# Three equal blocks in every slot, a lag of three, and weights laid out beforehand, in a three-stage decoder layer

## The chip, the cores and the metric

One core of a Trainium2 chip runs the whole program. Its engines are TensorE (PE; its weight loads are shown apart as PEld), VectorE (DVE), ScalarE (ACT), GpSimd (POOL) and SyncE (SP), which only issues transfers here. The metric is the device time of one execution in microseconds (us), as the median over runs; lower is better.

## What is computed

The input x has 16 batches of 128 rows of 256 numbers. Three blocks follow one another, each on the layer-normed x and added to x:

```python
x = x + attn(layernorm(x))          # 16 heads of 64; q, k, v, dots, weights, out are cut to 1/4096 and clipped at 8
x = x + xattn(layernorm(x), ctx)    # 16 heads; keys and values from a context of 128 rows of 128
x = x + ffn(layernorm(x))           # two experts share wi (1024) and wo; each adds a rank-16 product inside the relu
```

The first attention cuts every intermediate to fixed point (`trunc(clip(t) * 4096) / 4096`): q, k, v, the scores, the softmax weights, the attended values and the projection.

## The kernel before, in words

**Numbers.** Matrix products need more precision than one pass of rounded operands gives, so each operand is split in a rounded high part (`_hi`) and a low part (`_lo`, raw minus high), and a product is three matmuls (`split3`, lines 402 to 407: weights low by moving high and so on). A weight matrix must thus be transposed where its layout asks for it, rounded, and subtracted.

**Tiling.** Four groups of four batches (512 tokens). Stage A is the first attention, stage B the attention to the context, stage C the feed-forward part. In A and B a group is eight slots, a slot is two heads; in C a slot is 128 of the 1024 hidden columns. Each engine has its own program, and all walk through the same slots (`a_slot`, `b_slot`, `c_slot` in each engine's block); the first group is written out, the other three are a loop. The order inside a slot is written by hand for each engine, and counting semaphores tie the engines together. Each engine takes its instructions in strict order.

**Stage A, PE (lines 505 to 531).** A slot n makes the q block and the k block (128 weight columns by 512 tokens, six matmuls of 512 columns each, into PSUM banks `proj_ps[m % 2]`); transposes the weights of slot n-2 (`a_transpose`, L464); adds slot n-3's part to the output projection (`project_out`, 12 matmuls of 256 columns); attends for slot n-2 (`a_attend`, L475); in slots 0 to 3 only, makes two value blocks (`a_block`, one batch by 512 value columns each); and makes the scores (`a_scores`, L498). In slot 7 the next group's normalised rows are transposed (`normed_T`, L438) between projection and attend. So a slot has four blocks in 0 to 3 and two in 4 to 7 (`block_index`, lines 69 to 74).

**Stage A, the others.** Each block's result goes to ACT for its sign (`sign_of`, L804) and to DVE, which subtracts half the sign and writes int16 (`fix_blocks`, L1021), then clips (L1025). The bank is free when the integers are written (`a_ri`). Scores: sign (L851), integers (L1116), clip (L1120), exponential with sums (ACT, L819), reciprocal (DVE, L1047), then GpSimd makes the integer weights p_int (L311, L316), PE transposes them, ACT makes `aT_sb` of them (L809), and only behind that, on ACT, come the next slot's exponentials. `e_sb`, `p_int`, `rsum` and `rsc` are single. After the attend: sign (L826), integers (L1037), high part (L1040), low part (L1042). DVE also does the layer norm of the next group (L966, L978, L985, L1013) and the last rounding of the projection (`y_out` L1056, `fix_y` L1065 to L1071), GpSimd the root of the variance (L304, L306) and the sum into x (L325).

**Stage B** (PE lines 614 to 683, DVE 1147 to 1227) works alike without fixed point: maxima (L1164), negated (L1168), exponentials (ACT, L889), reciprocal (L1199), GpSimd's p_f (L363), transposes (L583), DVE's copies (L1175), attend (L595), high part on ACT (L900), low part on DVE (L1206). All blocks (q, value, k, value) go through one PSUM bank, `one_ps`: q is copied out by ACT (L875), k and values by DVE (L1145, L1137), each before the next block. A slot's order on PE is q, transposes, value, projection, k, attend, value, scores; slots 4 to 7 have no value blocks. Each group starts with four transposes of the context (L621).

**Weights.** Stage A's (`w_qkv`, `w_proj`) come in rows; PE transposes them (`a_weights_T`, L426) in 16 pieces, ACT rounds each to the high part (L791), DVE makes the low part (L1005); eight pieces stand before the first rows. The first DMA on SP's queue is 512 KB of these weights, the second the first group's rows. Stage B's high parts are converted by GpSimd's own DMAs (L343), the raw ones come through `raw_b`, and GpSimd subtracts (L351), in groups 0 and 1. Stage C's are transposed between B and C in 13 pieces (`c_weights`, lines 691 to 716, 910 to 929, 1237 to 1260), with the drain slots of stage B among them.

## Time and profile before

| | |
|---|---|
| runs | 730.95 us median of 3 (729.81 to 731.84) |
| profiled execution, span | 730.2 us; its own time is not given apart from the three runs, the median is 0.75 us above the span |
| busy share of the span | PE 92%, PEld 76%, DVE 75%, ACT 57%, POOL 37% |
| data moved in the first 1/40 of the span | 312 GB/s |
| DMA | 18.75 MB in all |

PE's busy time is from the start of a matmul to a modelled end, so that matmuls overlap in it; the distance between the starts of two matmuls tells what one costs. An idle time stands in brackets behind an instruction, with the engine and the instruction that ended it.

### The profile page before, as it was taken

Reading aid. Unit: us, or ns where it says so; the run is one execution under the profiler, and the core shown is the slowest. Engines: PE = TensorE matmul, PEld = TensorE weight load, DVE = VectorE, ACT = ScalarE, POOL = GpSimd, SP = SyncE. Lnnn points to the kernel's source line nnn. Section 1 sums busy time; section 2 is a strip of 40 time slices with the busy share of each in tenths; the row PEclk is TensorE's granted clock in tenths of the full one; section 3 lists DMA queues with packets and bytes.
Section 4 is the critical chain, followed back from the end, with each engine's and each line's share of the span. In section 5 each row is a group of like instructions: output and inputs, shape, how many; then the busy total and the mean of one; then the engine's idle time right before and its main releaser. Section 6 shows DMA issues by size and latency. Waiting matters only on the chain.

```text
span 730.2 us, 15676 instructions
## 1 busy us (share of the span) xinstructions
PE 672.8 (92%) x5186; PEld 551.7 (76%) x5186; DVE 550.0 (75%) x1142; ACT 413.7 (57%) x1443; POOL 272.6 (37%) x610
## 2 busy tenths in 40 slices
PE   5998879989998899878989999999999889999997
PEld 4777768777886788766777877787788777888986
DVE  5879887887888789757767776677667668787775
ACT  4677756767776777764455455445544563433432
POOL 1166754454445534535354344234333532010110
PEclk9999999999999999999999999999999999999999
DMA  9135100000000000050000000000000000000000
GB/s 312 49 111 150 60 30 1 1 1 1 0 0 0 0 0 0 0 153 1 1 2 16 1 1 1 14 0 0 0 0 0 0 1 1 2 30 0 29 29 29
DMA packets 17002, 18.75 MB, mean 26 GB/s; under 512 B 2851, under 2 KB 15427, under 8 KB 16963
## 3 DMA queue, kind: packets, MB, share of 16 engines
q1 hardware_dynamic: 15330, 15.11, 6.4%
q0 software_dynamic: 1632, 3.15, 1.5%
q8 instruction: 21, 0.34, 0.2%
q14 instruction: 19, 0.15, 0.1%
HBM read 16.16 MB, written 2.10 MB: 25 GB/s over the span
## 4 chain that ended last, share of the span: by engine, by line
PE 35%; POOL 7%; DVE 6%; ACT 3%; issue 3%; DVEq 0%; POOLq 0%; ACTq 0%
PE bank L405 9%; PE bank L407 8%; PE bank L406 8%; POOL p_f L363 6%; PE bank L583 3%; ACT e_sb L889 2%; PE bank L595 2%; PE bank L607 1%; DVE mx L1164 1%; PE bank L729 1%; PE bank L741 1%; DVE bn_st L966 1%; DVE oT_lo L1206 1%; POOL p_int L316 0%; DVE v_sb L1137 0%
## 5 line engine op out<-in xcount | busy, mean ns | idle before, releaser
L363 POOL TENSOR_SCALAR p_f<-e_sb,rsum 128x128 f32<-128x128 f32 x256 | 95.6, 398 | 156.7 <-DVE rsum L1199 156.7
L316 POOL TENSOR_SCALAR p_int<-e_sb,rsc 128x128 int16<-128x128 f32 x256 | 116.2, 475 | 6.3 <-issue 5.7
L889 ACT ACTIVATE e_sb<-bank,neg_max 128x128 f32<-128x128 f32 x256 | 90.1, 380 | 12.1 <-DVE neg_max L1168 11.9
L804 ACT ACTIVATE sgn<-bank 128x512 bf16<-128x512 f32 x96 | 57.2, 598 | 57.6 <-PE bank L407 57.6
L819 ACT ACTIVATE e_sb<-si 128x128 f32<-128x128 int16 x256 | 75.1, 303 | 0.0
L1021 DVE SCALAR_TENSOR_TENSOR ri<-sgn,bank 128x512 int16<-128x512 bf16 x96 | 62.5, 677 | 7.3 <-ACT sgn L804 6.5
L875 ACT COPY q_sb<-bank 128x512 f32<-128x512 f32 x32 | 18.8, 587 | 84.5 <-PE bank L407 84.5
L311 POOL TENSOR_TENSOR rsc<-rsum,growth 128x8 f32<-128x8 f32 x32 | 6.7, 209 | 156.0 <-DVE rsum L1047 156.0
L889 ACT ACTIVATION_READ_ACCUMULATOR e_sb<-bank,neg_max 128x1 f32 x256 | 55.9, 218 | 0.0
L405 PE MATMUL bank<-xnT_hi,wqkvT_lo 128*128 128x512 f32 x128 | 53.6, 419 | 2.2 <-DVE ri L1021 1.3
L1175 DVE COPY aT_sb<-bank 128x512 f32<-128x512 f32 x64 | 41.2, 685 | 12.7 <-PE bank L583 12.5
L407 PE MATMUL bank<-xnT_hi,wqkvT_hi 128*128 128x512 f32 x128 | 50.2, 392 | 0.0
L406 PE MATMUL bank<-xnT_lo,wqkvT_hi 128*128 128x512 f32 x128 | 49.9, 390 | 0.0
L819 ACT ACTIVATION_READ_ACCUMULATOR e_sb<-si 128x1 f32 x256 | 49.9, 195 | 0.0
L809 ACT ACTIVATE aT_sb<-bank 128x1024 f32<-128x1024 int16 x32 | 32.8, 1026 | 25.6 <-PE bank L464 25.6
L1145 DVE COPY k_sb<-bank 128x512 f32<-128x512 f32 x32 | 22.1, 691 | 30.0 <-PE bank L407 30.0
L583 PE MATMUL bank<-ident,p_f 128*128 128x128 f32 x256 | 34.1, 276 | 11.3 <-POOL p_f L363 10.5
L583 PEld LDWEIGHTS bank<-ident,p_f 128*128 128x128 f32 x256 | 28.5, 140 | 20.1 <-POOL p_f L363 15.4
L950 ACT CAST oT_hi<-hid 128x512 fp32r<-128x512 f32 x32 | 19.9, 622 | 41.0 <-DVE hid L1282 41.0
L1164 DVE TENSOR_REDUCE mx<-bank 128x4 f32<-128x512 f32 x64 | 40.8, 677 | 0.4
L464 PE MATMUL bank<-ident_b,p_int 128*128 128x128 bf16 x256 | 19.8, 220 | 22.7 <-POOL p_int L316 22.7
L405 PE MATMUL bank<-wpT_hi,oT_lo 128*128 128x256 f32 x128 | 39.1, 305 | 1.8 <-DVE oT_lo L1042 1.8
(162 smaller groups left out, 2039.5 us busy)
## 6 DMA issues: line engine op xcount, KB each, us to landing
x_sb<-in_x SPq DMA_DIRECT2D x4, 512.0 KB, 10.3
wqkv_raw<-in_L_attn_w_qkv SPq DMA_DIRECT2D x2, 1024.0 KB, 10.2
out<-x_sb SPq DMA_DIRECT2D x8, 256.0 KB, 2.2
wqkv_raw<-in_L_attn_w_qkv SPq DMA_DIRECT2D x2, 512.0 KB, 5.1
wp_raw<-in_L_attn_w_proj SPq DMA_DIRECT2D x1, 1024.0 KB, 12.3
raw_b<-in_L_xattn_Wq SPq DMA_DIRECT2D x2, 512.0 KB, 3.3
wq_hi<-in_L_xattn_Wq POOLq DMA_DIRECT2D x2, 512.0 KB, 4.1
wo_hi<-in_L_xattn_Wo POOLq DMA_DIRECT2D x2, 512.0 KB, 8.4
```

Source lines behind the costliest of these rows:

```text
L316: i = nc.gpsimd.tensor_scalar(p_int[:, t, :], e_sb[:, t, :], rsc[:, t:t + 1], -0.5, ALU.mult, ALU.add)
L363: i = nc.gpsimd.tensor_scalar(p_f[:, t, :], e_sb[:, t, :], rsum[:, t:t + 1], 0.0, ALU.mult, ALU.add)
L405: pe.matmul(out_, wl, mh, start=first, stop=False, **kw)
L406: pe.matmul(out_, wh, ml, start=False, stop=False, **kw)
L407: return pe.matmul(out_, wh, mh, start=False, stop=last, **kw)
L583: last = pe.transpose(pT_ps[hh][:, b * P:(b + 1) * P], p_f[:, GB * hh + b, :], ident[:, :])
L804: nc.scalar.activation(sgn[:, m % 2, :], proj_ps[m % 2][:, :], ACT.Sign).then_inc(a_sgn, 1)
L819: last = nc.scalar.activation(e_sb[:, t, :], si[:, i, j * P:(j + 1) * P], ACT.Exp, scale=1.0 / FIX, accum_out=sums[:, t:t + 1])
L889: last = nc.scalar.activation(e_sb[:, t, :], s_ps[hh][:, (t % 4) * P:(t % 4 + 1) * P], ACT.Exp, bias=neg_max[:, t:t + 1], scale=DH ** -0.5 ...
L1021: V.scalar_tensor_tensor(ri[:, i, :], sgn[:, i, :], -0.5, proj_ps[i][:, :], ALU.mult, ALU.add).then_inc(a_ri, 1)
L1164: V.reduce_max(mx[:, half], s_ps[hh][:, :].rearrange("p (a t) -> p a t", a=GB), AX).then_inc(b_mx, 1)
L1175: i = V.tensor_copy(aT_sb[:, GB * hh:GB * hh + GB, :].rearrange("p a t -> p (a t)"), pT_ps[hh][:, :])
```

## The change

In stages A and B every slot now makes three blocks: q, k and one value block, which is a quarter of the value columns (256) for two batches, side by side in one bank. Transposes and attend are for the slot three back (`LAG`), the projection for the slot four back, and `e_sb`, `p_int`, `p_f`, `rsum` and `rsc` are double. The host lays out the weights and the context transposed, so that no weight or context is transposed on PE; high parts come by GpSimd's DMAs (the first q, k and value pieces are rounded on ACT), low parts are made by GpSimd in halves of 512 (A) or pieces of 1024 (B and C, and the low rank factors). The scale of 4096 goes from the weights to the norm factor of the rows (one more small GpSimd product). The first group's rows are the first DMAs, on two queues, and PE runs 14 matmuls on zeros before anything has landed.

PE, stage A and B:

```diff
-    return 4 * s if s < 4 else 16 + 2 * (s - 4)
-BLOCKS = block_index(8)
+BLOCKS = 3 * NP
+LAG = 3
...
+            for _ in range(14):
+                pe.matmul(t_ps[:, :], warm[:, 0:P], warm[:, :], start=True, stop=True)
...
+            def a_rows(g, s):
+                m = 3 * s + 2
+                a_block_free(g, m)
+                for i in range(2):
+                    b = 2 * (s % 2) + i
+                    for kt in range(KD):
+                        last = split3(proj_ps[m % 2][:, i * QW:(i + 1) * QW],
+                                      [t[:, kt, b * P:(b + 1) * P] for t in (xnT_hi, xnT_lo)],
+                                      [w[:, s // 2, kt, :] for w in (wv_hi, wv_lo)], i == 0 and kt == 0, kt == KD - 1,
+                                      skip_group_check=True)
+                last.then_inc(a_blk, 1)
...
-                a_block(g, base, s * P, True)
-                a_block(g, base + 1, E + s * P, True)
...
-                    a_transpose(n - 2)
-                if not (first and s < 3):
-                    project_out(n - 3, (s - 3) % NP, a_olo, a_pj, (wpT_hi, wpT_lo), (a_z, 2 * g))
+                for i in range(2):
+                    a_block(g, 3 * s + i, [w[:, s, :, i, :] for w in (wqk_hi, wqk_lo)])
+                lagged = not (first and s < LAG)
+                if lagged:
+                    a_transpose(n - LAG, (s - LAG) % 2)
...
+                a_rows(g, s)
+                if lagged:
...
+                    a_attend(n - LAG, p, BLOCKS * gg + 6 * (p // 2) + 6)
                 if s == NP - 1:
-
                     normed_T(g + 1, lambda: wait(pe, a_ri, BLOCKS * (g + 1)))
...
+                    project_out(n - LAG - 1, p, a_olo, a_pj, (wp_hi, wp_lo), (a_z, 2 * g))
+                a_scores(n, s, BLOCKS * g + 3 * s + 2)
...
+                    b_block(g, s, "q")
+                    transposes()
+                    b_block(g, s, "v")
+                    project((0, 1))
+                    b_block(g, s, "k")
+                    project((2, 3))
+                if s == NP - 1:
...
+                    normed_T(G + g + 1, free)
+                attend()
+                b_scores(g, n, s)
...
-            for s in range(2):
+            for s in range(LAG):
                 b_slot(G, s, drain=True)
```

GpSimd, and the queues:

```diff
+            for b in range(2):
+                sp.dma_start(x_sb[:, b, :], x[b]).then_inc(ld_x0[b], 16)
+            sp.dma_start(wqk_raw[:, 0, :, :, :], wqk[:, 0, :, :, :]).then_inc(ld_qk[0], 16)
...
+            for b in range(2, GB):
+                nc.scalar.dma_start(x_sb[:, b, :], x[b]).then_inc(ld_x0[b], 16)
...
+                nc.gpsimd.tensor_tensor(lo, raw, hi.bitcast(F32), ALU.subtract).then_inc(w_lo, 1)
...
+            for part in LOW_ORDER[1:6]:
+                load_high(*part)
...
+            inv_std(0, scaled=True)
+            pool.wait_ge(ln_xn, 1)
+            for part in LOW_ORDER[0:3]:
+                make_low(*part)
...
+                if not first and s in (3, 6):
+                    chunk = 2 * (g - 1) + (s - 3) // 3
...
+                    nc.gpsimd.tensor_tensor(lo, raw, hi.bitcast(F32), ALU.subtract).then_inc(wB_done, 1)
...
+                    nc.gpsimd.tensor_tensor(wi_lo[:, s - 1, :], wi_raw[:, s - 1, :], wi_hi[:, s - 1, :].bitcast(F32),
+                                            ALU.subtract).then_inc(cw_lo, 1)
...
+                    nc.gpsimd.tensor_tensor(wd_lo[:, half, :], wd_raw[:, half, :], wd_hi[:, half, :].bitcast(F32),
+                                            ALU.subtract).then_inc(cw_lo, 1)
```

ACT and DVE, stage A (the high part of the attended values goes from DVE, L1040, to ACT):

```diff
+                    a_exp(n - 1, (s - 1) % 2, 0)
+                sign_of(g, 3 * s + 2)
+                if lagged:
+                    a_out_sign(n - LAG)
+                if s == NP - 1:
+                    xnT_high(g + 1)
+                if not (first and s == 0):
+                    a_exp(n - 1, (s - 1) % 2, 1)
+                if lagged:
+                    a_out_high(n - LAG)
...
                 between_groups(g, s, first)
+                to_int(g, 3 * s + 2)
...
+                    a_out(n - LAG)
+                clipped(g, 3 * s + 2, v_rows(s), ri[:, s % 2, :].rearrange("p (a c) -> p a c", a=2), 1.0)
                 if s == NP - 1:
                     xnT_low(g + 1)
                 if not (first and s == 0):
-                    a_recip(n - 1)
...
+                    a_recip(n - 1, (s - 1) % 2)
+                if lagged:
+                    a_out_low(n - LAG)
+                if s == LAG and not first:
                     y_out(g)
```

## Rows read from the trace of the kernel before

**Rows 1.** The page, busy time and instructions of each engine.
```profile
PE 672.8 (92%) x5186; PEld 551.7 (76%) x5186; DVE 550.0 (75%) x1142; ACT 413.7 (57%) x1443; POOL 272.6 (37%) x610
```

**Rows 2.** Timeline of PE: start us, us, instruction; row transposes, then stage C's first matmul.
```profile
14.78 1.52 PE L438 MATMUL bank<-ident,xn 128*128 128x128 f32 x8
...
86.32 0.93 PE L438 MATMUL bank<-ident,xn 128*128 128x128 f32 x7
...
165.23 1.04 PE L438 MATMUL bank<-ident,xn 128*128 128x128 f32 x8
...
314.59 1.04 PE L438 MATMUL bank<-ident,xn 128*128 128x128 f32 x8
...
388.63 1.09 PE L438 MATMUL bank<-ident,xn 128*128 128x128 f32 x8
...
586.77 1.09 PE L438 MATMUL bank<-ident,xn 128*128 128x128 f32 x8
...
609.13 0.47 PE L405 MATMUL bank<-xnT_hi,wiT_lo 128*128 128x512 f32 x1
```

**Rows 3.** Timeline of PE, one slot with values and one without, stage A.
```profile
202.88 0.62 PE L464 MATMUL bank<-ident_b,p_int 128*128 128x128 bf16 x8
203.31 0.36 PE L405 MATMUL bank<-wpT_hi,oT_lo 128*128 128x256 f32 x1
...
204.91 1.09 PE L475 MATMUL bank<-aT_sb,v_sb 128*64 128x128 f32 x16
205.93 0.50 PE L405 MATMUL bank<-wqkvT_hi,xnT_lo 128*128 128x512 f32 x1
...
208.92 1.16 PE L498 MATMUL bank<-k_sb,q_sb 64*128 64x128 f32 x16
...
212.91 0.62 PE L464 MATMUL bank<-ident_b,p_int 128*128 128x128 bf16 x8
...
221.29 0.62 PE L464 MATMUL bank<-ident_b,p_int 128*128 128x128 bf16 x8 [1.20 <-POOL p_int L316]
```

**Rows 4.** Timeline of POOL and DVE near 85; then line 1282: min/median/max ns, first and last start.
```profile
84.30 2.39 POOL L351 TENSOR_TENSOR wv_lo<-raw_b,wv_hi 128x1024 fp32r<-128x1024 f32 x1
...
85.29 1.68 DVE L1025 TENSOR_SCALAR q_sb<-ri 128x512 f32<-128x512 int16 x1
86.89 0.41 DVE L1025 TENSOR_SCALAR k_sb<-ri 128x512 f32<-128x512 int16 x1
...
L1282 DVE SCALAR_TENSOR_TENSOR hid<-relu,top_sb,hid x32: 741/750/822, 614.2 to 722.2; 128x512 f32<-128x512 f32 x32
```

**Rows 5.** Timeline of PE, the stall in group 1 of stage A.
```profile
106.70 0.62 PE L464 MATMUL bank<-ident_b,p_int 128*128 128x128 bf16 x8 [2.69 <-POOL p_int L316]
```

**Rows 6.** Timeline of PE, from transposes to transposes, a slot without values, stage B.
```profile
427.94 1.03 PE L583 MATMUL bank<-ident,p_f 128*128 128x128 f32 x8
...
435.63 1.10 PE L583 MATMUL bank<-ident,p_f 128*128 128x128 f32 x8 [0.81 <-POOL p_f L363]
```

**Rows 7.** Timeline of PE and DVE, the loop of a slot with values, stage B.
```profile
405.49 0.44 PE L405 MATMUL bank<-cT_hi,wk_lo 128*128 128x512 f32 x1
...
406.32 1.10 PE L595 MATMUL bank<-aT_sb,v_sb 128*64 128x128 f32 x16
...
408.96 0.68 DVE L1206 TENSOR_TENSOR oT_lo<-bank,oT_hi 128x512 fp32r<-128x512 f32 x1
...
410.21 1.27 DVE L1164 TENSOR_REDUCE mx<-bank 128x4 f32<-128x512 f32 x2
...
413.13 0.68 DVE L1137 COPY v_sb<-bank 128x512 f32<-128x512 f32 x1
...
413.93 0.44 PE L405 MATMUL bank<-cT_hi,wk_lo 128*128 128x512 f32 x1
```

**Rows 8.** Timeline of DVE, the first rows' statistics and their normalisation.
```profile
5.84 1.40 DVE L966 BATCH_NORM_STATS2 bn_st<-x_sb 128x6 f32<-128x256 f32 x4 [5.84 <-DMA x_sb<-in_x]
...
9.26 1.38 DVE L985 TENSOR_SCALAR xn<-x_sb,mv,rstd 128x256 f32<-128x256 f32 x4 [1.59 <-POOL rstd L306]
```

862 lines of the change are left out of this document (401 added, 461 removed).

## The prediction, made before the changed kernel was run

> **What bounds the kernel now.** I read the page first: TensorE (PE) is busy for 672.8 us, 92% of the span [rows 1]. That only says that PE is close everywhere, so I next cut the span into stages by one landmark, the transposes of the next group's normalised rows, which stand once in each group's pass [rows 2]. The first pass of stage A takes 86.32 - 14.78 = 71.5 us, the second 78.9, the next two together 149.4 (74.7 each); the first pass of stage B 74.0, the next three 198.1 (66.05 each); from the last landmark of stage B to the first matmul of stage C are 22.4 us. Stage C is not changed and its PE is never free, so it counts nothing.
>
> In a stage A group the first four slots take 10.03 us and have no gap; the last four wait for GpSimd's weights, 1.20 us in the slot shown (8.38 us long) [rows 3]. Three of these and one like it at the next group's first slot are all that lags can win: about 4.9 us a group. In stage B the gap before the transposes of an attend-only slot is 0.81 us [rows 6], while the slots with values run at the pace of a loop through VectorE (DVE): value copy, k block, attend, rounding, maxima, copies, next value copy; k to k is 8.44 us [rows 7].
>
> **Stage A, a slot of the new kernel.** The slot keeps everything of a 10.03 us slot but the two value blocks (12 matmuls of 512 columns, 2.99 us); it gets 12 of 256 columns. The projection is 12 matmuls of 256 columns and takes 1.60 us with its changeover [rows 3], and I take that. New slot: 10.03 - 2.99 + 1.60 = 8.64 us of pure PE. Eight of them and the landmark's 1.0: 70.1, where the old group has 74.7 - 4.9 = 69.8. So quarters cost PE 0.3 a group, and the gain is the gap alone. The Trainium skill, TensorE: Matmul & The Clock Gate, section Back-to-back issue gap, gives N/2.4 + 2.5 ns per matmul, 109 ns at 256 columns; by it twelve take 1.31 us, the slot 8.35, and four groups of stage A 9 us less. The row has 1.60, and the sum goes by the row.
>
> Where do new waits come from? A bank is free again after DVE has made integers of it, and with three blocks in two banks the value block of a slot waits for that slot's own q. By passes of 0.6 us, scores, sign, integers, clip and then q's integers end some 4.3 us after the scores' start, which is q's start + 3.2; PE comes there at +3.3. It holds with nothing to spare. Four things eat into it. The rows' transposes now stand behind the attend and need the last value block's integers: 1.05 us a group. The two output passes after the fourth slot's rounding: 0.75. The longer norm work of the second and fifth slot: 0.1. And GpSimd's own weight subtractions, next.
>
> **GpSimd holds DVE.** While GpSimd ran a subtraction of 2.39 us from 84.30, a DVE clip of an SBUF tile that started at 85.29 took 1.68 us where the next one took 0.41, that is, until GpSimd's was over; a DVE operation with two SBUF inputs took at most 0.82 against a median of 0.75 [rows 4]. In the old kernel six such subtractions stand in the first two groups. In the new one there are 14 half-wide ones in group 0, six full ones in groups 1 to 3 (two each, in slots 3 and 6), and some seven in the first pass of stage B. A held clip costs between 0 and 2.4 us; I charge 1.0 each, a little under the 1.27 that the row shows, because some will fall in a gap. Groups 1 to 3 get 2.0 each. The Trainium skill, GPSIMD Engine Reference, section 8. Key points, says that the two engines contend over DVE's two-port mode and over two SBUF inputs; by it roundings and sums would be held too, and the sum would be some 12 us more. By that rule, the trace agrees on the clip, and hardly on the two inputs (0.82 against 0.75).
>
> Sum for a group of A: 70.1 + 1.05 + 0.75 + 0.1 + 2.0 = 74.0. Against 78.9 in group 1, which also has a stall of 2.69 us behind GpSimd's subtractions [rows 5], -4.9. Groups 2 and 3: 148.0 against 149.4, **-1.4**. The cast that goes from DVE to ScalarE (ACT), some 0.5 us, I cost at nothing: ACT has over a microsecond free in such a slot. If that cover went, it would be 0.5 a slot.
>
> **Start and group 0.** Now the rows land at 5.84, behind 512 KB of weights, and DVE's normalised rows are ready at 10.64, but PE is still transposing weights and turns to them only at 14.78 [rows 8, 2]. The weight transposes, the 32 passes of ACT and DVE over their results, and PE's wait go. Rows asked for first should land about 1.6 us earlier (an estimate: 512 KB stand ahead of them, and the page's first slice moved 312 GB/s); one small GpSimd product costs 0.3. The landmark comes at 10.7 - 1.6 + 0.3 = 9.4: **-5.4**. Six DMA issues on GpSimd stand ahead of the root of the variance and should be over before it; if not, this term loses 1 to 3 us. The 14 warming matmuls lie in PE's idle time and cost nothing.
> Group 0: 2.7 to the first q; three slots with no attend, where the scores wait for k's passes, 6.7 each; 7.0 for the fourth (no projection); three of 8.64; 6.95 up to the landmark: 62.6. GpSimd's 14 subtractions of some 1.2 us hold clips while nothing else is slack: +4, bounds 0 to 12. So 67.0 against 71.5, **-4.5**.
>
> **Stage B.** A group has 7.69 - 0.81 = 6.88 us of PE in an attend-only slot [rows 6]; a value block of quarters is six matmuls of 256 columns, 0.80, and the split projection has one more changeover: 7.7. But now every slot has a value copy, and half a projection (0.80) stands between k and attend, inside DVE's loop. The old loop, 8.44, has 0.65 of statistics and a wait of 0.24 in it [rows 7]; without them 7.55. The second value block's copy leaves it: from attend to rounding it took 2.64, where attend, ACT's cast and their latencies need 1.8. New loop: 7.55 + 0.80 - 0.84 = 7.5, and every other DVE pass between rounding and maxima comes on top. By passes of 0.6 (512 wide) and 0.33 (256 wide) these are 0.6, 0.65, 1.85, 0.95, 1.25 and 0.65 in six of the slots. Over 7.7 that is 0.4 + 0.45 + 1.65 + 0.75 + 1.05 + 0.45 = 4.75. A group: 8 x 7.7 + 1.05 + 4.75 = 67.4 against 66.05: three groups **+4.1**. Stage B gets slower: its PE gap goes and a DVE wait takes its place.
> The first pass of B loses its context transposes and their stall, but takes over stage A's last three attends, and gets GpSimd's weight work. Without holds 67 to 68, with seven holds of about 1: 74 to 75 against 74.0: **0**, bounds -7 and +8.
>
> **From B to C.** Now 609.13 - 586.77 = 22.4 us [rows 2], full of the last stage's weight preparation on PE, ACT and DVE. New: 2.05 to the last scores, then maxima, exponentials, reciprocal, GpSimd's weights (8.9 us, in which two drain slots run on PE), transposes, projection, attend, low rank product and last projection, 6.5: 17.5. **-4.9**. Should GpSimd's preparation be late, this term is lost first; it has a whole stage of slack.
>
> **Sum.** -5.4 - 4.5 - 4.9 - 1.4 + 0 + 4.1 - 4.9 = -17.0. The profiled span is 730.2, 0.1% under the runs' median of 730.95; the profiled execution's own time is not given apart, so I put what lies around the span at the difference, 0.75: 730.95 - 17.0 = **714.0 us**. This case's own range is 703 to 725, chance 0.58.
>
> **Rivals.**
> (a) PE stays filled. Holds fall in gaps and DVE's passes fit. Then A groups are 70.1, B groups 62.7, the first passes lose 4 and 5 more: -11.7 - 4 - 14.1 - 5 = -34.8, 679 us. For it: DVE is idle a quarter of the span. Against it: strict order on each engine, and the loops above. Chance 0.13, most of it short of the full gain.
> (b) Slower. The place is the value block's wait for its slot's q. All of DVE's extra passes of a group (some 8.4 us) then lie on the loop, not the 0.85 charged, and a hold costs its whole length: +9 us a group, four times, 750 us. It decides from 0.53 us a slot more than forecast (17.0 over 32 slots). For it: the loop has 0.1 us to spare. Against: most extra passes stand where DVE waits for ACT's value sign. Chance 0.12.
> (c) The start doesn't deliver. Raw and rounded copies of 7 MB are asked for at once on three queues; rows or first weights land late. The 5.4 go and group 0 loses 4: 723. Chance 0.10.
> (d) GpSimd's subtractions hold DVE's two-input passes too: each of some 27 then also stops a rounding or sum, for about 0.45 more on average: 726. The row with 0.82 against 0.75 speaks against it [rows 4]. Chance 0.07. It is what the page of the Trainium skill on GPSIMD, named above, would have.
>
> **How the numbers follow.** A difference of 0.3% (2.2 us) is about what can be told from no change. 690 to 733 leaves out most of (b) and the far end of (a). Faster: 0.56 of the forecast's 0.58, all of (a), about 0.13 of (c) and (d) together: 0.82. Within 0.3%: 0.04. Slower: 0.14.
>
> **What the profile after would show.** Right: the first landmark near 9.4; landmarks in stage A 74 apart with slots of 8.6 to 8.7, no wait of transposes for GpSimd, PE's waits being on DVE's integers; clips lengthened to 1 to 2.4 us beside GpSimd's subtractions; stage B's landmarks 67 apart with k waiting for the value copy; 17.5 us from the last to stage C. Wrong: slots of A over 9.2 all along (b), B at 63 (a), a first landmark after 13 (c), long roundings (d).

## The result and the profile after

The changed kernel takes **741.6 us** (median of 4 runs, 739.9 to 742.7) where the kernel before takes 730.8 beside it: ratio 1.0148, 95% interval 1.0133 to 1.0164. I forecast 714.0 with a range of 690 to 733 and gave "slower" 0.14. It is slower, and outside the range.

The page of the profile, busy time by engine, against [rows 1]:

```profile
PE 671.4 (91%) x5358; PEld 569.2 (77%) x5358; DVE 533.4 (72%) x1080; ACT 413.8 (56%) x1445; POOL 307.8 (42%) x656
```

PE is busy 1.4 us less and the span is 9.3 us longer (739.5 against 730.2). The 1.4 hides two things. The mean granted clock fell from 0.995 to 0.979: ahead of the end seven stretches, 30.7 us in all, ran at half clock (1.2 GHz), where a matmul counts for longer; before there were two of 3.4 us. And work did leave PE: kernel 11 below, with the same matmuls and eight more, is busy for 658.1 us at a mean clock of 0.995 again, 14.7 less than before (its order differs too). So what was won on PE went into waits and half clock. Where, the windows between landmarks tell. The columns are: stretch, its length, PE busy (instructions), weight loads, DVE, ACT, POOL, granted clock as a share of the full one, DMA share, GB/s. The rows are the start, stage A's four groups, stage B's four, the passage to C, and C to the end.

```profile
0.00:12.11 12.11, 4.87 (x14) 1.74 (x15) 4.01 (x15) 2.42 (x3) 6.44 (x21) 0.98 0.84 251
12.11:83.47 71.36, 62.65 (x468) 51.66 (x469) 50.81 (x106) 46.62 (x158) 44.47 (x77) 0.91 0.51 190
83.47:160.22 76.75, 71.50 (x617) 61.27 (x617) 62.06 (x127) 57.28 (x194) 36.50 (x78) 0.98 0.01 2
160.22:237.48 77.26, 71.89 (x617) 61.33 (x617) 62.60 (x127) 57.52 (x194) 37.86 (x79) 0.98 0.00 0
237.48:313.20 75.72, 70.39 (x616) 60.06 (x617) 62.49 (x127) 57.43 (x194) 37.86 (x79) 1.00 0.02 4
313.20:392.17 78.97, 66.20 (x540) 55.47 (x541) 52.94 (x103) 40.57 (x163) 48.11 (x96) 0.96 0.18 62
392.17:462.43 70.26, 64.76 (x544) 55.08 (x545) 45.85 (x100) 33.77 (x147) 30.39 (x70) 0.98 0.02 5
462.43:531.15 68.72, 63.21 (x545) 53.82 (x545) 45.73 (x100) 33.88 (x147) 24.72 (x66) 1.00 0.02 4
531.15:599.87 68.72, 63.19 (x544) 53.78 (x545) 45.72 (x100) 33.86 (x147) 24.71 (x66) 1.00 0.00 0
599.87:618.65 18.78, 17.15 (x167) 14.80 (x167) 9.93 (x19) 6.79 (x23) 5.61 (x16) 1.00 0.00 1
618.65:739.50 120.85, 115.60 (x692) 100.15 (x690) 91.28 (x165) 43.68 (x75) 11.17 (x10) 1.00 0.05 18
```

Against [rows 2] and my terms (us, after minus before):

| stretch | before | after | difference | forecast |
|---|---|---|---|---|
| start | 14.78 | 12.11 | -2.7 | -5.4 |
| A, group 0 | 71.54 | 71.36 | -0.2 | -4.5 |
| A, group 1 | 78.91 | 76.75 | -2.2 | -4.9 |
| A, groups 2 and 3 | 149.36 | 152.98 | +3.6 | -1.4 |
| B, group 0 | 74.04 | 78.97 | +4.9 | 0 |
| B, groups 1 to 3 | 198.14 | 207.70 | +9.6 | +4.1 |
| B to C | 22.36 | 18.78 | -3.6 | -4.9 |
| C | 121.07 | 120.85 | -0.2 | 0 |

The first two rows are less sure than they look. Six more traces (experiments 1 to 5 and 9) have the changed kernel's own program up to the second landmark, and reach it at 84.0 to 87.6 us, the first at 11.5 to 13.9. One trace tells the start and group 0 together to some 4 us, no better. A later group of the same program mostly repeats within 0.3 us, or within 1 to 2 where a stretch at half clock moves in or out.

Every term but C's missed to the same side, and the waits of PE say by what (line waited at, what was waited for: us in total, times, longest):

```profile
PE bank L464 <- DVE v_sb L1117: 26.2, 27, 3.7
PE bank L464 <- DVE ri L994: 14.3, 7, 2.9
PE bank L479 <- DVE ri L994: 8.2, 4, 2.4
PE bank L479 <- DVE xn L968: 5.9, 1, 5.9
```

The first is stage B's key block behind the value copy, 27 times. The second and third are stage A's value blocks (and one query block in group 0) and row transposes behind the integers. The fourth is the start. GpSimd's weights, for which PE waited before [rows 3, 5, 6], are gone from this list: the lag of three slots did what it is for.

**Stage A: the hold.** The timeline of slot 3 to 4, group 1 (start, duration, engine, instruction, wait in brackets):

```profile
121.96 1.28 DVE L1038 TENSOR_TENSOR raw_b<-bank,bias_a 128x512 f32<-128x512 f32 x2
...
123.16 1.27 DVE L1096 SCALAR_TENSOR_TENSOR si<-s_sgn,bank 128x512 int16<-128x512 bf16 x2
...
124.35 2.85 DVE L1100 TENSOR_SCALAR si<-si 128x512 int16<-128x512 int16 x2
...
124.67 2.38 POOL L348 TENSOR_TENSOR wB_lo<-wB_raw,wB_hi  x1
127.12 1.27 DVE L994 SCALAR_TENSOR_TENSOR ri<-sgn,bank 128x512 int16<-128x512 bf16 x2
...
127.85 0.58 PE L464 MATMUL bank<-wv_hi,xnT_lo 128*128 128x256 f32 x1 [2.85 <-DVE ri L994]
```

Two score clips that take 0.49 us together elsewhere take 2.85, until GpSimd's subtraction ends at 127.05. The query's integers stand behind them, and PE's value block behind those. The clock is granted at full speed (2.4 GHz) up to 127.6 and at half of it (1.2 GHz) for the 3.4 us behind PE's wait:

```profile
124.40:127.60 3.20, 0.60 (x9) 1.00 0.00 0
127.60:131.00 3.40, 3.15 (x16) 0.50 0.00 0
```

Here a held clip is paid more than once: its own length, the wait at the row transposes (2.39 us instead of 1.09 in group 0, from the second subtraction) and a slow stretch of clock.

**Stage B: the short cover.** A plain slot, group 1. PE's value block ends and half a projection runs; DVE is still on the second copy of transposed weights, and copies the values from 407.06 on:

```profile
405.62 0.38 PE L464 MATMUL bank<-wB_hi,cT_lo 128*128 128x256 f32 x1
405.86 1.29 DVE L1155 COPY aT_sb<-bank 128x512 f32<-128x512 f32 x2 [0.60 <-PE bank L624]
406.44 0.28 PE L464 MATMUL bank<-wB_hi,oT_lo 128*128 128x256 f32 x1
...
407.06 0.68 DVE L1117 COPY v_sb<-bank 128x512 f32<-128x512 f32 x1
407.80 0.50 PE L464 MATMUL bank<-cT_hi,wB_lo 128*128 128x512 f32 x1 [0.48 <-DVE v_sb L1117]
```

From key block to key block a plain slot is 8.23 us (407.80 to 416.03), where I had 7.7. In the slot behind the additions (427.98 on) the wait is 1.91 us, because bias sums, statistics and moments stand ahead of that same copy.

### The profile page after: what moved, and what is told of

It is laid out like the page before. It is cut to its first block, busy times and chain, and to the rows that moved or that the text cites. A ratio compares the mean times of both kernels' runs of the same rounds, so it can differ in the third digit from the quotient of the medians.

```text
span 739.5 us, 16172 instructions
## 1 busy us (share of the span) xinstructions
PE 671.4 (91%) x5358; PEld 569.2 (77%) x5358; DVE 533.4 (72%) x1080; ACT 413.8 (56%) x1445; POOL 307.8 (42%) x656
## 4 chain that ended last, share of the span: by engine, by line
PE 67%; DVE 15%; issue 7%; ACT 6%; DMA 2%; SPq 2%; DVEq 1%; ACTq 0%
PE bank L464 17%; PE bank L465 14%; PE bank L466 14%; PE bank L636 5%; PE bank L547 4%; PE bank L524 3%; PE bank L648 3%; DVE v_sb L1117 3%; PE bank L624 2%; DMA x_sb<-in_x 2%; ACT e_sb L818 2%; DVE mx L1144 2%; DVE aT_sb L1155 2%; PE bank L479 1%; DVE ri L994 1%
## 5 line engine op out<-in xcount | busy, mean ns | idle before, releaser
L327 POOL TENSOR_SCALAR p_int<-e_sb,rsc 128x128 int16<-128x128 f32 x256 | 108.1, 441 | 6.3 <-issue 5.9
L994 DVE SCALAR_TENSOR_TENSOR ri<-sgn,bank 128x512 int16<-128x512 bf16 x96 | 65.1, 682 | 35.4 <-ACT sgn L803 34.4
L464 PE MATMUL bank<-xnT_hi,wqk_lo 128*128 128x512 f32 x128 | 54.1, 423 | 3.9 <-DVE ri L994 2.4
L1185 DVE TENSOR_TENSOR oT_lo<-bank,oT_hi 128x512 fp32r<-128x512 f32 x32 | 22.1, 692 | 44.4 <-ACT oT_hi L905 44.4
L905 ACT CAST oT_hi<-bank 128x512 fp32r<-128x512 f32 x32 | 18.8, 587 | 60.6 <-PE bank L636 60.6
L464 PE MATMUL bank<-wv_hi,xnT_lo 128*128 128x256 f32 x128 | 40.2, 314 | 12.2 <-DVE ri L994 11.9
L466 PE MATMUL bank<-xnT_hi,wqk_hi 128*128 128x512 f32 x128 | 50.9, 398 | 0.0
L465 PE MATMUL bank<-xnT_lo,wqk_hi 128*128 128x512 f32 x128 | 50.8, 397 | 0.0
L1096 DVE SCALAR_TENSOR_TENSOR si<-s_sgn,bank 128x512 int16<-128x512 bf16 x64 | 41.0, 682 | 6.6 <-ACT s_sgn L853 6.2
L853 ACT ACTIVATE s_sgn<-bank 128x512 bf16<-128x512 f32 x64 | 34.7, 594 | 12.6 <-PE bank L547 12.6
```

Source lines behind the costliest of these rows:

```text
L327: i = nc.gpsimd.tensor_scalar(p_int[:, half, t, :], e_sb[:, half, t, :], rsc[:, half, t:t + 1], -0.5, ALU.mult, ALU.add)
L464: pe.matmul(out_, wl, mh, start=first, stop=False, **kw)
L465: pe.matmul(out_, wh, ml, start=False, stop=False, **kw)
L466: return pe.matmul(out_, wh, mh, start=False, stop=last, **kw)
L994: V.scalar_tensor_tensor(ri[:, m % 2, :], sgn[:, m % 2, :], -0.5, proj_ps[m % 2][:, :], ALU.mult, ALU.add).then_inc(a_ri, 1)
L1096: V.scalar_tensor_tensor(si[:, i, :], s_sgn[:, i, :], -0.5, s_ps[i][:, :], ALU.mult, ALU.add).then_inc(a_si, 1)
```

## The experiments

Each run is the changed kernel with the edit shown, unless it says otherwise; 741.6 us is what the first ones are compared with. The ratios are to the kernel before, run beside each.

**1. The whole projection between value and key block.**

```diff
-                    project((0, 1))
+                    project()
                     b_block(g, s, "k")
-                    project((2, 3))
```

> The changed kernel (741.6 us) with one edit: in the slots 1 to 7 of stage B the whole projection (12 matmuls, 1.4 us) stands between the value block and the key block, as it did before, instead of half ahead of the key block and half behind. Theory 1 (the quarter of values is too short a cover for the one bank's copy): the key block's wait of 0.48 us in each plain slot goes, and 0.7 us of the longer waits; 7 slots by about 0.55 in each of four groups is 15 us, so about 726, and a plain slot of 7.76 instead of 8.24 us. Rival (the slot is held by the DVE or ACT loop, and the wait only moves to the scores or the attends): 738 to 742, with a new wait ahead of the scores.

Measured: 725.8 us, ratio 0.9945 (0.9928 to 0.9963). Stage B's groups:

```profile
388.93:453.36 64.43, 62.05 (x544) 52.71 (x545) 46.14 (x100) 33.87 (x147) 30.88 (x70) 1.00 0.02 5
453.36:517.77 64.41, 62.03 (x544) 52.71 (x545) 45.97 (x100) 33.90 (x147) 24.75 (x66) 1.00 0.01 4
```

64.4 us for a group instead of 68.7 to 70.3. The plain slot is 7.52 us (scores at 406.47 and 413.99), shorter than the 7.76 I expected: the rows' "0.48" counts from the end that is modelled for the last matmul, and wait and split together were worth 0.71. The scores do not wait for the key copy. The split itself costs PE a little too, as experiment 2 shows. Theory 1 holds, and this edit alone makes the changed kernel faster than the one before.

**2. The same wait, met from DVE's side.** PE's order stays; on DVE the value copy stands between the two copies of weights.

```diff
                         i = V.tensor_copy(aT_sb[:, GB * hh:GB * hh + GB, :].rearrange("p a t -> p (a t)"),
                                           pT_ps[hh][:, :])
+                        if hh == 0 and not drain:
+                            v_ready(g, s, first)
+                            b_v_rows(g, s)
                     i.then_inc(b_pT, 1)
...
-                    b_v_rows(g, s)
+                    if not lagged:
+                        v_ready(g, s, first)
+                        b_v_rows(g, s)
```

> The changed kernel, TensorE's order untouched (half the projection ahead of the key block, half behind); on DVE the value copy stands between the two copies of the transposed weights instead of behind them. Theory 1 (the key block waits for DVE's queue order: the copy starts 0.46 us after the value block's end because the second copy of weights is ahead): the copy ends at 0.7 us after the block instead of 1.15, 0.45 us less in each plain slot, 12 to 14 us, about 728. Rival (the cover is simply too short, the latency of one copy from a bank is what is waited for, whatever stands ahead): 739 to 742.

Measured: 724.7 us, ratio 0.9915 (0.9899 to 0.9932). The value block ran from 405.94. Its copy, half a projection's last matmul and the key block:

```profile
406.95 0.69 DVE L1117 COPY v_sb<-bank 128x512 f32<-128x512 f32 x1
...
407.36 0.28 PE L466 MATMUL bank<-wB_hi,oT_hi 128*128 128x256 f32 x1
...
407.70 0.50 PE L464 MATMUL bank<-cT_hi,wB_lo 128*128 128x512 f32 x1
```

The copy now starts as soon as the block ends, and a plain slot is 7.82 us (407.70 to 415.53): 0.41 of the wait was DVE's queue order, as theory 1 had it. But the slot is not 7.52. The matmul at 407.36 could be followed 0.12 us later, and the key block starts 0.34 later, when the copy has ended at 407.64. So some 0.22 us of wait is the rival's: one copy takes longer than half a projection. In the changed kernel the same reckoning (407.04, 407.80) gives 0.64 of wait. What is left, 7.60 against 7.52, is the price on PE of splitting the projection. That the two runs' times are alike (725.8 and 724.7) is partly chance: stage B's four groups take 264.4 us in experiment 1 and 267.6 here (286.7 in the changed kernel), while the profiled execution of experiment 1 reached the second landmark 3.4 us later, with no edit there.

**3. DVE's additions into its own gap.** In stage B the bias and residual sums, statistics and normalizing move from behind the output's low part to ahead of it (where DVE waits for ACT's copy), and the moments behind the key copy.

```diff
-                if s == 4 and not drain:
-                    norm_moments()
...
                     b_k_rows(g, s)
+                if s == 4 and not drain:
+                    norm_moments()
...
-                if lagged:
-                    wait(dve, b_ohi, n - LAG + 1)
-                    V.tensor_tensor(oT_lo[:, :], o_ps[:, :], oT_hi[:, :].bitcast(F32), ALU.subtract).then_inc(b_olo, 1)
                 if s == LAG and not first:
...
                     norm_apply(G + g + 1, (g + 1) % G, (ln_T, 2 * (G + g) + 2), (0, 1) if s == 5 else (2, 3))
+                if lagged:
+                    wait(dve, b_ohi, n - LAG + 1)
+                    V.tensor_tensor(oT_lo[:, :], o_ps[:, :], oT_hi[:, :].bitcast(F32), ALU.subtract).then_inc(b_olo, 1)
```

> The changed kernel with one edit: in stage B's slots DVE's additional work (the bias and residual sums, the statistics, the normalizing) stands behind the reciprocal, where DVE waits 1.56 us for ACT's copy of the attend's output, instead of behind the low part of that output; the statistics' combination behind the key copy. Theory 1 (the additions delay the maxima, and with them the copies that free the bank): the key block's waits in slots 4 and 6 fall from 1.91 and 0.94 us to the 0.48 of a plain slot, and the slow clock stretch behind the first goes; about 6 to 7 us, so 735. Rival (the low part of the output is itself needed at once, its delay stops the next slot's projection): no gain or a loss, 741 to 744.

Measured: 729.1 us (10 runs), ratio 0.9990 (0.9975 to 1.0004), twice the expected gain. Groups 1 to 3 take 66.8 each, which is the 1.9 us (3.5 in group 1, which also lost its slow stretch of clock) that I expected. The rest is group 0, 72.9 instead of 79.0: with the additions out of the way two of the four maxima pairs no longer met GpSimd's subtractions for stage C, and two slow clock stretches became one. I had left group 0 out.

**4. GpSimd's low parts moved, first try.**

```diff
-                if not first and s in (3, 6):
-                    chunk = 2 * (g - 1) + (s - 3) // 3
+                if not first and s in (0, 3):
+                    wait(pool, a_fx, BLOCKS * g + 3 * s + 2)
+                    chunk = 2 * (g - 1) + s // 3
```

> The changed kernel with one edit: GpSimd's subtraction for stage B's low parts (2.4 us, two in each of stage A's groups 1 to 3) stands in the slots 0 and 3 instead of 3 and 6, and waits there until DVE has done the slot's key clip, so that it runs in the 2.4 us in which DVE clips nothing. Theory 1 (the hold on DVE's one-input passes is what stops PE): the value block's wait of 2.85 us in slot 4 goes, the wait ahead of the row transposes falls from 2.39 to about 1.1 us, and with them the slow stretch of the clock behind the first; 3 x (2.85 + 1.3) + 1.8 = 14 us, so about 727. Rival (DVE's own extra work, y_out in slot 3, is what is late, the hold only shows in it): the wait in slot 4 stays at over 1.2 us, and 735 to 737.

Measured: 741.7 us, ratio 1.0151 (1.0115 to 1.0187): nothing. The rows say why:

```profile
126.71 0.72 POOL L327 TENSOR_SCALAR p_int<-e_sb,rsc 128x128 int16<-128x128 f32 x2
127.06 2.85 DVE L1101 TENSOR_SCALAR si<-si 128x512 int16<-128x512 int16 x2
...
127.39 2.37 POOL L349 TENSOR_TENSOR wB_lo<-wB_raw,wB_hi  x1
```

On GpSimd the subtraction of "slot 3" stands behind that slot's weights pass, which needs a reciprocal that DVE makes after the clip I waited for. The wait was long fulfilled, and the subtraction fell on the same two clips. Only the row transposes gained (1.00 instead of 2.39 us); a value block in another slot now waits 0.56. The test was not of the theory but of a wrong place.

**5. The same, ahead of the weights pass.** The two lines above stand before `a_weights` instead of after it.

> The changed kernel with GpSimd's six subtractions for stage B placed ahead of its weights pass in the slots 0 and 3, behind a wait for the slot's key clip. The earlier try stood behind that pass, 3.4 us later than the window: its trace shows the subtraction from 127.39 to 129.77 us on top of DVE's two score clips (2.86 us for the pair), and the wait of 2.86 us at the value block as before, while the wait at the row transposes fell to 1.00. Theory 1 (the hold alone): the value block's wait in slot 4 goes, with the slow clock stretch behind it, and the row transposes wait 1.0 us: 3 x (2.85 + 1.3) + 1.8 = 14 us, about 727. Rival (y_out's 1.28 us in DVE's queue makes a wait by itself): about 1.2 us stay in slot 4, 731.

Measured: 726.3 us, ratio 0.9942 (0.9920 to 0.9965). Stage A's groups 1 to 3:

```profile
85.29:157.13 71.84, 70.16 (x617) 60.02 (x617) 57.93 (x127) 57.33 (x194) 36.19 (x78) 1.00 0.01 2
157.13:229.36 72.23, 70.38 (x617) 60.06 (x617) 58.63 (x127) 57.46 (x194) 37.50 (x79) 1.00 0.00 0
229.36:301.55 72.19, 70.38 (x616) 60.06 (x617) 58.67 (x127) 57.46 (x194) 37.46 (x79) 1.00 0.00 1
```

4.9, 5.0 and 3.5 us less, where I had charged 2.0 for the two holds. The value block of slot 4 waits 0.68 us instead of 2.85: that is what y_out's place costs by itself, so the rival explains a quarter of the wait and the hold the rest.

```profile
127.51 0.39 PE L465 MATMUL bank<-wv_hi,xnT_lo 128*128 128x256 f32 x1 [0.68 <-DVE ri L995]
```

These groups are 13.4 us of the 15.3. In the profiled execution stage B's first group is 3.2 shorter too, with one stretch at half clock instead of two.

**6. Later row transposes in stage A.**

```diff
-                if s == NP - 1:
-                    normed_T(g + 1, ...)
                 if not (first and s <= LAG):
                     ...
                     project_out(...)
+                if s == NP - 1:
+                    normed_T(g + 1, ...)
```

> The changed kernel with one edit: in slot 7 of stage A the next group's row transposes stand behind the output projection instead of ahead of it, so that 1.6 us of other matmuls lie between the last value block and the transposes that need its integers. Theory 1 (the wait of 1.09 us in group 0 and of 2.39 in the others is cover that is missing): the wait goes in group 0 and falls to 0.8 in the others; a wait of some 0.4 us appears ahead of the next group's query block, whose rows come later. 0.6 + 3 x 1.2 = 4 us, about 737.5. Rival (the query block behind waits for just as long as was saved): 741 to 742.

Measured: 742.4 us, ratio 1.0158 (1.0116 to 1.0200). The rows of group 2's beginning:

```profile
162.69 1.09 PE L479 MATMUL bank<-ident,xn 128*128 128x128 f32 x8 [0.80 <-DVE ri L994]
165.34 0.50 PE L464 MATMUL bank<-xnT_hi,wqk_lo 128*128 128x512 f32 x1 [0.47 <-DVE xnT_lo L988]
169.63 0.39 PE L464 MATMUL bank<-wv_hi,xnT_lo 128*128 128x256 f32 x1 [0.82 <-DVE ri L994]
```

0.80 and 0.47 as I had worked out, and 0.82 at the next value block on top: what was saved is waited for one block later. The rival is right, though by one more step than it named.

**7. The start: rows normalized first.**

```diff
             norm_moments()
+            norm_apply(0, 0, (ln_T, 0))
             dve.wait_ge(w0_hi, 1)
             ...
-            norm_apply(0, 0, (ln_T, 0))
```

> The changed kernel with one edit at the start: DVE normalizes the first rows before it makes the first weights' low part, instead of behind it. Theory 1 (the rows are there early, but DVE's queue stands behind the weights): the first row transposes start at about 9.0 instead of 12.1 us, the first query block at 12.4 instead of 15.5, so about 738.5. Rival (the start is held by the weights' transfers, which land at 9.3 us and later, and the first slots wait for the low parts then): the transposes come early but the block does not move by more than 1 us, 741.

Measured: 742.4 us, ratio 1.0166 (1.0145 to 1.0186). The transposes start at 9.05 and the first query block at 12.47, both as expected, and the second landmark is where it was (84.08 against 83.47). One row shows where it went:

```profile
32.00 0.29 DVE L1078 TENSOR_SCALAR bias_a<-bias_a 128x256 f32<-128x256 f32 x1 [4.49 <-DMA x_sb<-in_x]
```

**8. The start again**, with experiment 7's edit, that wait (and the first group's statistics and moments) one slot later and 22 matmuls of warming instead of 14.

```diff
-                if first and s == 1:
+                if first and s == 2:
                     dve.wait_ge(ld_b, 16)
                     ...
-            for _ in range(14):
+            for _ in range(22):
```

> The start again: rows normalized ahead of the weights' low part, as in the run that gave nothing; and, new, DVE waits for the other groups' rows in slot 2 instead of slot 1 (the first group's statistics and moments a slot later), and 22 instead of 14 matmuls of warming. The trace of the run that gave nothing has the transposes at 9.05 and the query block at 12.47 us as expected, but DVE then stands from 27.5 to 32.0 us in slot 1, and TensorE 2.1 us with it, and 6.8 us of half clock begin at 9.5. Theory 1 (the early start was lost in those): no half clock between 9 and 16 us, no stand at 27.5; the first group ends 4 to 5 us earlier (second landmark 79 instead of 83.5), 737. Rival (the first group is paced by the fourteen subtractions of weights on GpSimd and what they hold on DVE): second landmark at 83 to 84, 741.

Measured: 737.5 us, ratio 1.0073 (1.0048 to 1.0099), the time of theory 1, though not in its place: the second landmark came at 81.5, not at 79, and the query block at 13.63, since the first weights landed later (their rounding at 10.20 against 9.04). Of the half clock ahead of 16 us, 3.4 us were left (13.5 to 16.9). Traces with this start (experiments 8, 10 and 11) reach the second landmark at 80.3 to 81.5 us, those with the changed kernel's at 83.5 to 87.6 (median 84.2): some 3 of the 4.1 us lie there.

**9. Stage B's two edits together** (1 and 3).

> Both edits of stage B together (the whole projection ahead of the key block; DVE's additional work in its gap behind the reciprocal). Alone they gave 725.8 and 729.1 us from 741.6. Theory 1 (two different waits, the plain slot's and that of the slots with additions): the plain slot stays at 7.52 us, the 1.2 us wait that was left in slot 4 and the slow clock stretches in group 0 go; a group of 62 us instead of 64.4, group 0 67 instead of 71.2, so about 715. Rival (the gap behind the reciprocal is only 0.85 us in the shorter slot, the additions no longer fit): the low part comes late and the gain of the second edit is halved, 720.

Measured: 715.9 us, ratio 0.9782 (0.9747 to 0.9817). Groups of 62.7, 62.5 and 62.5 us; with 8 slots of 7.52 and the row transposes that is nearly PE's own work (61.6 busy). Stage B's group 0 took 70.0, where I had expected 67. In the slot with the additions the low part follows directly behind the last of them, and nobody waits for it.

**10. All of them** (1, 3, 5 and 8).

> Stage B's two edits, the low parts in the window, and the start, all in one kernel. Alone they gave 25.7, 15.3 and 4.1 us. Theory 1 (separate waits, each paid once): 741.6 - 45.1 = 696.5 us. Rival (the slow clock stretches were counted in more than one of them, or the same DVE queue limits what is left): 702 or more.

Measured: 695.8 us, ratio 0.9508 (0.9488 to 0.9528). The parts add up to within 0.7 us, so the waits were separate ones.

**11. Two more edits of the same kind**, on top of 10. The second half of y_out behind the next slot's clips; stage C's weight subtractions ahead of GpSimd's pass, behind the negated maxima:

```diff
+                if first and 0 < s < 5:
+                    c_low_part(s)      # wait(pool, b_nm, 2 * s), then the subtraction
                 if not (first and s == 0):
                     b_weights(NP * g + s - 1, (s - 1) % 2)
```

> As the run with all of them, and two more edits of the same kind: the second half of y_out stands behind the next slot's clips, and GpSimd's four subtractions for stage C's weights in stage B's first group stand ahead of its weights pass, behind a wait for the slot's negated maxima. Theory 1: the value block's remaining 0.7 us in slot 4 of three groups goes, and in the first group of stage B the held maxima (1.5 to 2.2 us a pair) with the key block's wait of 1.94 and one slow clock stretch: 2 + 4 = 6 us less, about 690.5. Rival (the subtraction now delays the weights pass by 2.4 us, and the transposes three slots later wait for it): no gain, 696.

Measured: 692.9 us, ratio 0.9471 (0.9455 to 0.9487): half of what I expected. (The move of y_out's second half is not shown.) Stage A's groups 1 to 3 went from 72.1 to 71.5 on average, B's group 0 from 69.9 to 68.1.

**12. What is the third slot of lag worth?** Kernel 10, with one line changed:

```diff
-LAG = 3
+LAG = 2
```

> As the run with all of them, but transposes and attends lag two slots, as before, instead of three. What it tells is what the third slot is worth once the waits are gone. Theory 1 (the third slot is the cover for GpSimd's pass): in the profile of the changed kernel that pass ends 0.5 us after the place where the transposes of two slots' lag would stand in stage A, and in the shorter slot of stage B 0.5 us after too; 0.5 to 0.8 us in each of 60 slots is 30 to 50 us, less the two shorter drains, so 720 to 740. Rival (two slots are enough, the lag of three buys nothing): 694 to 698.

Measured: 734.6 us, ratio 1.0042 (1.0028 to 1.0056), that is 38.8 us more than with three. PE's waits of this kernel:

```profile
PE bank L514 <- POOL p_int L327: 18.9, 32, 2.7
PE bank L625 <- POOL p_f L384: 18.7, 30, 3.9
```

Both stages wait for GpSimd in nearly every slot again, 37.6 us in sum. That this is so near to the 38.8 is in part chance: the profiled execution took 740.4 us, with a mean clock of 0.978, and is 44.8 us longer than kernel 10's. The range and the mechanism are as theory 1 had them. The lag was a good part of the change, hidden by what came with it.

**13 to 16. What holds the start and group 0.** These four start from kernel 11 (692.9 us). First (13) the first weights ahead of the rows 0 and 1 on SyncE's queue:

```diff
+            sp.dma_start(wqk_raw[:, 0, :, :, :], ...)
             for b in range(2):
                 sp.dma_start(x_sb[:, b, :], x[b])...
-            sp.dma_start(wqk_raw[:, 0, :, :, :], ...)
```

> The best kernel so far (692.9 us) with one edit: on SyncE's queue the first query and key weights are issued ahead of the rows 0 and 1 instead of behind them. Open is why the start gave 2.7 instead of the 5.4 us I forecast and group 0 0.2 instead of 4.5: in every run the first query block stands 3.4 to 4.4 us behind the row transposes, and the weights' raw copy lands at 9.3 us or later. Theory 1 (the transfer's place in the queue is the bound now): the block starts at about 12.4 instead of 14.5 us, 690.8. Rival (all transfers share the same 16 engines in these 10 us, the place hardly counts, and the rows come later): first transposes at 10 or later, no gain, 692 to 694.

Measured: 695.1 us, ratio 0.9521 (0.9506 to 0.9535), 2.2 us more than kernel 11: the rival's side, and a little beyond it. The order swaps what is late:

```profile
4.25 0.62 ACT L796 CAST wqk_hi<-wqk_raw 128x512 fp32r<-128x512 f32 x1 [0.34 <-DMA wqk_raw<-in_wqk]
...
7.53 1.08 DVE L952 BATCH_NORM_STATS2 bn_st<-x_sb 128x6 f32<-128x256 f32 x3 [2.23 <-DMA x_sb<-in_x]
...
12.44 1.25 PE L483 MATMUL bank<-ident,xn 128*128 128x128 f32 x8 [3.73 <-DVE xn L971]
```

Then (14), with the weights first, group 0's own nine later subtractions in windows behind the key clips:

```diff
+                if first and 0 < s < 6:
+                    wait(pool, a_fx, 3 * s + 2)
+                    for part in LOW_ORDER[3 + 2 * s:5 + 2 * s]:
+                        make_low(*part)
                 if not (first and s == 0):
                     a_weights(NP * g + s - 1, (s - 1) % 2)
```

> As the run with the weights first, and the last nine of the fourteen subtractions of stage A's own weights go, two a slot in the slots 1 to 5 of group 0, ahead of GpSimd's weights pass behind a wait for the slot's key clip. Theory 1 (group 0, too, is slowed by what they hold on DVE): the waits ahead of the value blocks of the slots 1 to 5 (0.6 to 1.4 us each, 4.1 in all) mostly go, 3 to 4 us less than the run with the weights first. Rival (the subtractions now delay the weights pass by 2.6 us in each of five slots, or a low part is late for its block): no gain or up to 4 us more.

Measured: 694.3 us, ratio 0.9508 (0.9495 to 0.9521). Group 0 is 69.1 instead of 71.0 us in the profile, but its first landmark came 0.8 later; the two kernels' intervals overlap, so the 3 to 4 us expected did not come. The same windows with the rows first (15):

> The kernel of 692.9 us (rows first) with the windows of group 0 alone. With the weights first the two landmarks swapped: the first weights' copy was made at 4.25 instead of 10.35 us, but the last rows' statistics at 8.6 instead of 5.0, and the first transposes at 12.4 instead of 9.05; the windows took 1.9 us out of group 0. Theory 1 (order only swaps what is late; the windows' gain stays): 690 to 691.5. Rival (the windows' gain was a gain on the later start alone): 693.

Measured: 692.0 us, ratio 0.9478 (0.9462 to 0.9494); group 0 70.5 instead of 72.0. Against kernel 11 nothing can be told apart by the times. Last (16), no further weights issued until the first have landed:

```diff
             sp.dma_start(wqk_raw[:, 0, :, :, :], ...)
+            sp.wait_ge(ld_qk[0], 16)
             ...
+            pool.wait_ge(ld_qk[0], 16)
             for part in LOW_ORDER[0:2]:
                 load_high(*part)
             inv_std(0, scaled=True)
```

> As the run with rows first and windows in group 0, and SyncE and GpSimd issue no further weights until the first query and key weights have landed (some 2.5 MB in front of them or beside them no longer share the engines). Theory 1 (sharing is the bound of the start): the first weights land near 5 us with the rows, transposes at 9 to 9.5, first query block at 12 to 12.5 instead of 14.5 us; 2 us less than without, 689, if the later weights are still in time. Rival (the later weights, now 3 us later, stop the slots 1 to 3): the first group is not shorter, 691 to 694.

Measured: 697.1 us, ratio 0.9546 (0.9530 to 0.9562). The first weights' rounding stands at 7.06 us instead of 10.41, so the other transfers do delay this one, by some 3 us; but my wait stood ahead of the root of the variance on GpSimd, the rows came to the transposes at 11.93, and the later weights were late: group 0 took 75.2 us. That the start can be had by a better order of these transfers was not shown.

## Why the prediction was wrong, step by step

**What held.** Stage A's pure slot: 8.64 us forecast, 8.64 measured (query blocks at 95.62 and 104.26 us). Its 256-column matmuls start 0.12 us apart (119.74, 119.86, 119.98), so the row decided rightly against the 109 ns of the Trainium skill, TensorE: Matmul & The Clock Gate, section Back-to-back issue gap. The whole of stage A's sum but the holds held as well: without its 2.0 for them it says 72.0 us a group, and experiment 5, where they are gone, has 71.8, 72.2 and 72.2, with waits of 1.00 at the row transposes (1.05 charged) and 0.68 to 0.72 behind y_out (0.75 charged). So in these groups the holds alone were mis-sized. No transposes wait for GpSimd. The cast that moved to ACT shows in no wait of PE's, stage C is untouched, and B's groups 1 to 3 did get slower. The passage to C gave 3.6 of the 4.9 forecast. Held passes, and passes that are not held, of the changed kernel (min/median/max ns, first and last start); the last row is of experiment 7:

```profile
L1100 DVE TENSOR_SCALAR si<-si x64: 273/286/2427, 25.0 to 319.1; 128x512 int16<-128x512 int16 x64
L994 DVE SCALAR_TENSOR_TENSOR ri<-sgn,bank x96: 667/686/689, 19.1 to 312.5; 128x512 int16<-128x512 bf16 x96
L1025 DVE TENSOR_TENSOR oT_lo<-oi,oT_hi x32: 691/692/915, 50.6 to 343.8; 128x512 fp32r<-128x512 int16 x32
...
L1025 DVE TENSOR_TENSOR oT_lo<-oi,oT_hi x32: 691/692/1614, 48.9 to 345.1; 128x512 fp32r<-128x512 int16 x32
```

What is held is DVE's TENSOR_SCALAR on a tile in SBUF: clips, normalizing, negated maxima. Not every pass with one input is: the integers read one input from a bank and never took over 689 ns, and two passes of statistics (0.41 us each, at 335.57 and 335.90) kept their length beside a subtraction that began at 335.85. The third row reads two inputs from SBUF. In the changed kernel none of these 32 met a subtraction of GpSimd's. Where one did, it was held as the clips are: 1.60 to 1.62 us in experiments 3, 4, 5, 7 and 9 (fourth row), and 2.14 to 2.37 in kernel 11 and experiments 13 to 16. So the rule of the Trainium skill, GPSIMD Engine Reference, section 8. Key points, is borne out on two SBUF inputs too. It can also hit the other side: beside DVE's own two-input subtraction at 12.02 us GpSimd's took 1.79 us, where others of its size take 1.3. Rival (d) failed not because such passes are spared, as [rows 4] had suggested, but because they seldom met a subtraction.

**"Over 7.7 ... the loop 7.5" (stage B's base, +4.1).** The step that failed most; the holds, next, are the second. I checked PE's work against one loop through DVE, k to k, and shortened that loop by taking one copy out. I did not ask what stands ahead of the remaining value copy in DVE's queue: two copies of transposed weights that cannot start before the transposes end. The single bank makes PE wait for that copy in 27 of 32 slots. The base was 8.23, not 7.7: 7.60 of PE with its split projection, so that my PE term was 0.1 too high, and 0.64 of wait, which I had at nothing. Of it 0.41 is the queue order, and some 0.22 stays with the copy at the head of the queue (experiment 2): half a projection is too short a cover even then. The additions I had charged with 4.75 a group cost 1.9 (experiment 3). Two errors of opposite sign, 4.3 us a group too little and 2.9 too much, with 1.5 of slow clock in group 1.

**"I charge 1.0 each" (the holds).** 3.5 us a group at full clock, 4.9 to 5.0 with a slow stretch of clock, for two subtractions (experiment 5). A hold costs its whole 2.4 us where the clip stands ahead of the integers for which PE waits, and the additions of slot 3 put it there; the reason I gave for under-charging ("some will fall in a gap") was a hope, no row. Rival (b) had this mechanism and this place, with a price too high: 9 us a group, where the whole wait was 5.

**"Bounds -7 and +8" (B's group 0).** +4.9 came within the bounds. The holds there fall on the negated maxima, passes of 128 x 4 that I had not thought of as clips; experiments 3 and 11 took 6.1 and 1.8 us out. That the term came within its bounds says little for the forecast of 0: "without holds 67 to 68" fits kernel 11 (68.1), but the other 11 us were, for the most part, holds on four pairs of maxima, the value copy's wait and two stretches at half clock together, not seven holds of 1 us.

**"The landmark comes at 9.4" (start).** The rows did come early (statistics at 3.31 us, moments at 5.09, where [rows 8] has 5.84 for the first). DVE then stood 4.5 us at the first weights' low part with the rows' normalizing behind it in its program:

```profile
9.98 0.69 DVE L980 TENSOR_TENSOR wqk_lo<-wqk_raw,wqk_hi 128x512 fp32r<-128x512 f32 x1 [4.52 <-ACT wqk_hi L793]
```

I had read the old order into the new kernel, though the diff shows the new one. With the order turned the landmark is 9.05. But it bought nothing by itself: the first query block waits for the same weights, and group 0 for the rest.

**"So 67.0" (group 0 of stage A).** 71.4. A +4 for holds was in it; the transfers for slots 0 and 1, the wait for all other groups' rows in slot 1 (4.5 us of DVE, experiment 7) and half clock from 11.6 to 18.4 and, behind that wait, from 35.4 to 42.3 us were not. In experiment 8, with the wait a slot later, the second stretch is gone. How the remaining 3 to 5 us split between transfers and holds stays open: the windows took out 1.5 to 1.9 by the profiles (14 and 15), too little for the times to show.

**The range.** Rival (a) said 679 us if PE stays filled. Kernel 11 is that case with 692.9: A's groups at 71.3 to 71.7 (I had 70.1), B's at 62.5 (62.7). Some 9 of the 14 us between the two are group 0 of stage A, 72.0 where rival (a) has 63. It took edits of order alone and eight warming matmuls, no new data path. The rivals were the right ones; what was wrong is that I gave DVE's queue the benefit of the doubt at the places where PE had least to spare.

## What to carry to other kernels

When a block of matmuls is halved, ask what it was covering: on a single bank the copy behind it must end before the next block, and everything ahead of that copy in the copying engine's queue counts, as does the copy itself. Put an engine's extra work where that engine waits for somebody else, not where it is convenient in the program; here that alone was 12.5 us. And place GpSimd's long two-input work by DVE's schedule, behind a wait for the last DVE pass that it would hold, at the point of GpSimd's own program where that wait is still open.

## What the runs showed that I had not expected

- **A four-element pass is held like a wide one.** In stage B's group 0 two negations of 128 x 4 took 2.21 us beside a subtraction of 2.36, where 0.29 is usual; the copies from a bank right behind them took their normal 1.27 for two.

```profile
357.69 2.36 POOL L418 TENSOR_TENSOR wd_lo<-wd_raw,wd_hi 128x1024 fp32r<-128x1024 f32 x1
...
357.93 2.21 DVE L1148 TENSOR_SCALAR neg_max<-mx 128x4 f32<-128x4 f32 x2
...
360.06 1.27 DVE L1155 COPY aT_sb<-bank 128x512 f32<-128x512 f32 x2
```

- **GpSimd's one-input pass costs DVE little.** While it made weights from 112.82 to 116.24 us, in eight instructions, the two score clips took 0.49 together. Over the changed kernel no clip took more than 0.47 beside this pass, and a subtraction with two SBUF inputs 0.92 instead of 0.69 (at 343.80), while one of GpSimd's eight took 0.80 instead of 0.38. Whether the single input spares DVE, or only that each instruction is short, was not tested.

```profile
112.82 2.72 POOL L327 TENSOR_SCALAR p_int<-e_sb,rsc 128x128 int16<-128x128 f32 x6 [0.20 <-issue]
...
114.90 0.49 DVE L1100 TENSOR_SCALAR si<-si 128x512 int16<-128x512 int16 x2
```

- **Waits of PE come back as half clock.** The mean granted clock fell from 0.995 to 0.979 with the change, and is 0.995 again in kernel 11, whose only half-clock stretch before the end is the 6.8 us after 11.8. A stretch of 3.4 us cost a group 1.0 to 1.5 us (76.7 and 77.3 against 75.7 in stage A, 70.3 against 68.7 in stage B). Not every wait brings one: of stage B's three waits of 1.9 us, only the one before 433.93 did. Of the changed kernel's waits of 2.85 us the one at 127.85 had a slow stretch with it and the one in group 3 had none, so its cost differs from group to group (4.9 and 3.5 us).
